# Causal mask of the transposed scores: a minimum on VectorE for a product on TensorE, and the value products a slot later

## Chip, core and metric

One core of a Trainium2 chip runs the whole program. The metric is the device time of one execution, in microseconds (us). The engines are named as in the profile: PE is TensorE, DVE is VectorE, ACT is ScalarE, POOL is GpSimd, SP is SyncE, which here only issues DMAs.

## Reference

One transformer layer with a mixture of experts: attention with 16 heads of 8 columns over 16 sequences of 256 tokens, a layer norm, a top-1 choice among 8 experts, and a second layer norm. Cut to what matters here (written together, in the reference's terms):

```python
x = L0_attn_x                                        # (16, 256, 128), f32
q, k, v = (x @ w + b).reshape(B, S, 16, 8)           # for wq, wk, wv; then RoPE on q and k
scores = einsum('bhqd,bhkd->bhqk', q, k) / sqrt(8)
causal = where(tril(ones((S, S))) == 0, -1000000000.0, 0.0)
attn = softmax(scores + causal, axis=-1)
x = layernorm(x + einsum('bhqk,bhkd->bhqd', attn, v) @ wo + bo)
# top-1 of 8 experts, each takes at most T // 8 = 512 tokens in order; T = 4096
# (the shapes follow the reference's routing; tokens over the limit get zero)
out = gate * kept * (x @ W[e].T + b[e])
return layernorm(x + out)
```

## Kernel before

The work is cut by sequence. A sequence of 256 tokens passes through five stages, and a **step** s works on five or six sequences at once, each in another stage: n = s + 2 (projections and rotation), a = s + 1 and b = s (row maxima of the scores), c = s - 1 (scores again, exponentials, products with the values), d = s - 2 (norm, output projection, routing, experts), e = s - 3 (the last norm and output). There are 20 steps, s = -2 to 17; steps 1 to 16 have a sequence c.

Every step is cut into **slots** (14 of them, `SLOTS`), and each engine's program is the same loop over the slots with its own work written under them. That hand-written order is all that sets what an engine does next: no engine takes anything out of turn, and they meet in semaphores. Work that stands in an earlier slot is ahead in the queue of its engine, and in one slot the order is that of the code.

Attention is computed twice over. The first pass computes scores with a query a row and takes the row maxima (DVE, line 725), in eleven **chunks** k of up to 512 columns (`CHUNKS`). Each is a mask product (`masks`, line 898, with `mask_a_bf`), then products of the rotated queries and keys (line 924) into one of the two banks `ps_a`; PE waits in `a_taken` until DVE has taken chunk k - 2. The second pass computes the scores transposed, in the same eleven chunks, with the maxima already subtracted by extra rows of the product: a mask product (line 898, with `mask_b_bf`), which adds -3e9 where a key is behind its query, the products (line 914) into one of the two banks `ps_b`, and the exponential on ACT into one of the `PR` buffers of `probs` (line 544). Blocks have 64 tokens, so in each group of a chunk only the first 64 columns, the diagonal block, hold masked elements: 8 chunks have two groups (128 mask columns), 2 have four (256), the last has eight (512). Products of `probs` with the values (line 936, called PV k here) add up in `ps_pv`; a column of ones among the values gives the sums.

Chunk k of the second pass stands in slot k + 2 (`B_SLOT`), PV k in slot k + 3 (`PV_SLOT`). The maxima of b stand in the slots that `MAXIMA_IN` names, its chunk 2 in slot 0, chunk 3 in slot 2, chunk 4 in slot 3 and so on; chunks 0 and 1 of a are in the last two slots (`EARLY`). DVE has, besides the maxima: the reciprocals of the sums (lines 735, 737), attn (line 742), the choice of the largest among the experts' results (`select`, line 711), the residual sums and statistics (lines 704, 749, 691, 695), the splitting of x and of the normed rows (lines 763, 767), routing (lines 772 to 821) and the rotation products (lines 798, 801). POOL has the splitting of the rotated rows and maxima, the copies into `v_diag` and the reciprocal roots.

Of the kernel before, what the change touches and what calls it, by code (L numbers as in the profile page):

```python
# [27 lines left out]
B, S, D = 16, 256, 128  # L28
# [5 lines left out]
BLK = 64  # L34
# [18 lines left out]
NCH = len(CHUNKS)  # L53
B_SLOT, PV_SLOT, SLOTS = 2, 3, NCH + 3
EARLY = 2
# [3 lines left out]
def _layout():  # L59
    at = 0  # L60
    for name, w in (("ident", 128), ("before", 128), ("cos", S), ("sin", S), ("mask_a", BLK), ("mask_b", BLK),
                    ("stacked", BLK), ("head_cols", PH * HD), ("head_is", PH), ("tie", E), ("max_sel", H // 2)):
        CONSTS[name] = (at, w)
        at += w
    return at
# [23 lines left out]
def layer_kernel(nc, x, wq, bq, wk, bk, wv, bv, wo, bo, wg, W, b, const, expert_rows, out):  # L89
# [8 lines left out]
    with ExitStack() as ctx:  # L98
# [22 lines left out]
        out_bias = sb("out_bias", [128, 128])  # L121
        PR = 3
        probs = sb("probs", [128, PR, 512])
# [9 lines left out]
        ident_bf = sb("ident_bf", [128, 128], bf)  # L133
        mask_a_bf, mask_b_bf = sb("mask_a_bf", [128, BLK], bf), sb("mask_b_bf", [128, BLK], bf)
        stacked_bf = sb("stacked_bf", [128, BLK], bf)
# [64 lines left out]

        names += """b_ready exp_done pv_ready""".split()

# [286 lines left out]
        def _(act):  # L489
# [29 lines left out]
            def narrow_tables():  # L519

                act.wait_ge(s_["tables_loaded"], 16)
                for to, name in ((ident_bf, "ident"), (mask_a_bf, "mask_a"), (mask_b_bf, "mask_b"), (stacked_bf, "stacked"),
                                 (before_bf, "before")):
                    last = act.activation(to[:, :], C(name), ACT.Copy)
                last.then_inc(s_["consts_done"], 1)
# [8 lines left out]
            def step(s, p, half):  # L534
                n, a, b, c, d = s + 2, s + 1, s, s - 1, s - 2
                for slot in range(SLOTS):
# [31 lines left out]
                    if slot == 11 and has(b):  # L568
# [9 lines left out]
                        for half_at in range(2):  # L578
                            act.dma_start(q_plain[p][SCORE_ROWS:SCORE_ROWS + MAX_ROWS, 4 * half_at:4 * half_at + 4, :],
                                          max_rows[MAX_ROWS * half_at:MAX_ROWS * half_at + MAX_ROWS, :].unsqueeze(1)  # L580
                                          .broadcast_to([MAX_ROWS, 4, S])).then_inc(s_["maxrows_loaded"], 16)
                    if slot == 13 and has(c):
                        after(act, "pv_ready", c, NCH, NCH)
# [13 lines left out]
        def _(dve):  # L597
# [116 lines left out]
            def step(s, p, half):  # L714
                n, a, b, c, d, e = s + 2, s + 1, s, s - 1, s - 2, s - 3
                for slot in range(SLOTS):
                    for t, k in maxima_at(slot, a, b):
                        after(dve, "a_ready", t, NCH, k + 1)
# [12 lines left out]
                    if slot == 3 and has(e):  # L731
                        select(e, 1)
                    if slot == 13 and has(c):
                        after(dve, "sums_copied", c, 1, 1)
                        dve.reciprocal(inv_den[:, 0:128], sums[:, 0:128]).then_inc(s_["den_done"], 1)  # L735
# [101 lines left out]
        def _(pe):  # L837
# [62 lines left out]
            def step(s, p, half):  # L900
                n, a, b, c, d = s + 2, s + 1, s, s - 1, s - 2
                q = 1 - p
                for slot in range(SLOTS):
                    k = slot - B_SLOT
                    if has(c) and 0 <= k < NCH:
# [5 lines left out]
                        after(pe, "exp_done", c, NCH, k - 1)  # L911
                        masks(ps_b[k % 2], CHUNKS[k], mask_b_bf, False)
                        for j, g, col in parts_of(CHUNKS[k]):
                            mm = pe.matmul(ps_b[k % 2][:, col:col + width(j)], diag_block(k_diag[q], g, j),  # L914
                                           q_plain[q][:, g, BLK * j:S], start=False, stop=True, skip_group_check=True)
                        mm.then_inc(s_["b_ready"], 1)
# [23 lines left out]
                    if slot == 11 and has(b):  # L940
# [82 lines left out]
def constants():  # L1023
# [50 lines left out]
```

## Time and profile before

| what | value |
|---|---|
| time, median of 3 runs | 451.69 us (450.78 to 453.25) |
| profiled execution, its own time | 453.58 us |
| span of the profile | 451.9 us |
| PE busy | 407.0 us (90%) |
| DVE busy | 316.2 us (70%) |
| POOL busy | 202.9 us (45%) |
| ACT busy | 173.6 us (38%) |
| mean granted clock of PE | 0.947 of full speed |

The span runs from the first to the last instruction of the profiled execution; its own time is 1.7 us more. The busy share is a mean over start, middle and end: the middle, where all stages are full, is the part to read by windows. Matmuls are pipelined, so the length of one in the trace is longer than its share of PE: what one costs is the distance from its start to the start of the next. On DVE too the next instruction can start a little (some 0.08 us) before the end of the one ahead. A PE product of 4-byte data is two records in the trace.

### The profile page before, as it was taken

How to read it: one execution, taken by the hardware profiler on the slowest of the kernel's cores; microseconds unless marked ns; L12 is line 12 of the kernel's file. 1: busy time of each engine (PE TensorE's matmuls, PEld its weight loads, DVE VectorE, ACT ScalarE, POOL GpSimd, SP SyncE). 2: the span in 40 equal slices, each digit the busy share in tenths (PEclk: the TensorE clock that was granted, in tenths of full speed). 3: DMA queues.
4: the chain of work that ended last, by engine and by line, in shares of the span. 5: the costliest groups of instructions: out<-in, count | busy, mean ns of one | idle time of the engine just before them, and what ended most of it. 6: DMA issues, size and time to landing. Idle time of an engine off the chain costs nothing. (4 is left out here: it accounts for less than half of the span.)

```text
span 451.9 us, 10461 instructions
## 1 busy us (share of the span) xinstructions
PE 407.0 (90%) x3270; PEld 356.6 (79%) x3270; DVE 316.2 (70%) x814; ACT 173.6 (38%) x377; POOL 202.9 (45%) x376
## 2 busy tenths in 40 slices
PE   5363798999999999999999999999999999999842
PEld 4352687989898898989898989898898988897731
DVE  5567544768786878878787778786868877755553
ACT  7541234343444434434434343434434343435300
POOL 6265133333635354463646363635354555151313
PEclk9658696999999999999999999999999999999958
DMA  5399663928468684939393939587586759600000
GB/s 142 75 197 147 117 85 81 158 62 141 87 121 123 126 114 119 122 101 147 86 162 84 148 81 153 88 144 97 128 114 134 98 130 108 95 10 23 13 0 24
DMA packets 145828, 47.29 MB, mean 105 GB/s; under 512 B 104350, under 2 KB 142114, under 8 KB 145803
## 3 DMA queue, kind: packets, MB, share of 16 engines
q1 hardware_dynamic: 139898, 42.65, 58.1%
q10 hardware_dynamic: 5184, 2.36, 2.8%
q0 software_dynamic: 720, 1.97, 1.5%
q8 instruction: 13, 0.21, 0.2%
q14 instruction: 13, 0.10, 0.1%
HBM read 30.70 MB, written 14.68 MB: 100 GB/s over the span
## 5 line engine op out<-in xcount | busy, mean ns | idle before, releaser
L936 PE MATMUL ps_pv<-probs,v_diag 128*128 128x64 f32 (+3 forms) x1024 | 192.8, 324 | 2.9 <-ACT probs L544 2.4
L936 PEld LDWEIGHTS ps_pv<-probs,v_diag 128*128 128x128 f32 x1024 | 147.6, 193 | 12.6 <-ACT probs L544 6.7
L544 ACT ACTIVATE probs<-ps_ab 128x512 f32<-128x512 f32 (+1 forms) x176 | 97.8, 559 | 153.6 <-PE ps_ab L914 149.2
L725 DVE TENSOR_REDUCE row_max<-ps_ab 128x2 f32<-128x512 f32 (+3 forms) x176 | 107.9, 631 | 20.3 <-PE ps_ab L924 20.1
L924 PE MATMUL ps_ab<-k_plain,q_diag 128*128 128x64 bf16 (+3 forms) x512 | 67.0, 241 | 0.0
L914 PE MATMUL ps_ab<-q_plain,k_diag 128*128 128x64 bf16 (+3 forms) x512 | 65.3, 236 | 0.0
L898 PE MATMUL ps_ab<-mask_a_bf,ident_bf 128*128 128x128 bf16 (+2 forms) x176 | 44.6, 253 | 11.7 <-DMA q_diag<-plain_parts 8.1
L711 DVE TENSOR_REDUCE y_sel<-ps_m 128x128 f32<-128x1024 f32 x31 | 37.8, 1219 | 14.2 <-PE ps_m L887 14.2
L437 POOL COPY v_diag<-v_rows 64x128 f32<-64x128 f32 x64 | 18.4, 288 | 64.8 <-ACT v_rows L566 62.8
L898 PE MATMUL ps_ab<-mask_b_bf,ident_bf 128*128 128x128 bf16 (+2 forms) x176 | 43.7, 248 | 0.0
L914 PEld LDWEIGHTS ps_ab<-q_plain,k_diag 128*128 128x128 bf16 x512 | 36.1, 99 | 8.2 <-issue 0.6
L735 DVE RECIPROCAL inv_den<-sums 128x128 f32<-128x128 f32 x16 | 15.2, 953 | 37.1 <-ACT sums L508 37.1
L375 POOL TENSOR_SCALAR rs<-mv 128x2 f32<-128x2 f32 x32 | 7.3, 230 | 74.3 <-DVE mv L695 74.3
L924 PEld LDWEIGHTS ps_ab<-k_plain,q_diag 128*128 128x128 bf16 x512 | 37.0, 101 | 3.4
L898 PEld LDWEIGHTS ps_ab<-mask_a_bf,ident_bf 128*128 128x128 bf16 x176 | 17.9, 102 | 21.5 <-DVE row_max L725 7.8
L469 POOL TENSOR_TENSOR rot_rest<-rot 128x512 f32<-128x512 f32 x15 | 17.6, 1174 | 35.4 <-ACT rot L590 35.4
L798 DVE SCALAR_TENSOR_TENSOR rot_cs<-ps_m,bias_cols,cst 128x256 f32<-128x256 f32 x32 | 15.3, 479 | 17.6 <-PE ps_m L869 17.6
L867 PE MATMUL ps_m<-we_hi,x1t_hi 128*128 128x512 f32 x62 | 27.6, 445 | 0.0
L867 PE MATMUL ps_m<-xt_hi,w_hi 128*128 128x256 f32 x64 | 21.2, 331 | 4.7 <-DVE xt_lo L767 4.7
L466 POOL TENSOR_TENSOR rot<-rot_cs 128x512 f32<-128x512 f32 x15 | 19.4, 1296 | 13.1 <-DVE rot_cs L801 11.4
L386 POOL TENSOR_SCALAR y_out<-z,mv,rs 128x128 f32<-128x128 f32 x30 | 23.8, 795 | 3.4 <-POOL rs L377 3.4
L868 PE MATMUL ps_m<-we_lo,x1t_hi 128*128 128x512 f32 x62 | 25.0, 403 | 0.0
(156 smaller groups left out, 726.1 us busy)
## 6 DMA issues: line engine op xcount, KB each, us to landing
plain_parts<-rot SPq DMA_DIRECT2D x180, 64.0 KB, 2.0
k_plain<-plain_parts SPq DMA_DIRECT2D x16, 384.0 KB, 3.8
q_diag<-plain_parts SPq DMA_DIRECT2D x32, 192.0 KB, 5.3
q_plain<-plain_parts SPq DMA_DIRECT2D x16, 384.0 KB, 5.9
k_diag<-plain_parts SPq DMA_DIRECT2D x32, 192.0 KB, 6.6
x_in<-in_L_attn_x_dram SPq DMA_DIRECT2D x16, 128.0 KB, 5.9
x_res<-in_L_attn_x_dram SPq DMA_DIRECT2D x16, 128.0 KB, 3.0
out_dram<-y_out POOLq DMA_DIRECT2D x15, 128.0 KB, 2.6
```

Of the source, the lines that this page charges most:

```text
L386: last = pool.tensor_scalar(y_out[:, t, :], z2[:, t, :], mv2[:, t, 0:1], rs2[:, t:t + 1], ALU.subtract, ALU.mult)
L437: last = pool.tensor_copy(dst[:, :, :, HD * hl:HD * hl + HD], src[:, :, :, HD * hl:HD * hl + HD])
L466: pool.tensor_tensor(rot[:, :, :], rot_c[:, :, :], rot_s[:, :, :], ALU.add).then_inc(s_["rot_done"], 1)
L544: act.activation(probs[:, k % PR, 0:cols], ps_b[k % 2][:, 0:cols], ACT.Exp, scale=SCALE)\
L711: dve.tensor_reduce(y_sel[:, t, :], expert_bank(d, t)[:, :, :].rearrange("p a (e f) -> p f (a e)", e=4), AX.X, ALU.max).then_inc(s_["moe_t ...
L725: last = dve.tensor_reduce(row_max[:, NBLK - 1 - j, groups[0]:groups[-1] + 1], scores[:, :, col:col + width(j)], AX.X, ALU.max)
L867: pe.matmul(out, sh, mh, start=start, stop=False, skip_group_check=True)
L868: pe.matmul(out, sh, ml, start=False, stop=False, skip_group_check=True)
L898: return pe.matmul(v, ident_bf[:, :], rows, start=True, stop=False, skip_group_check=True)
L914: mm = pe.matmul(ps_b[k % 2][:, col:col + width(j)], diag_block(k_diag[q], g, j), q_plain[q][:, g, BLK * j:S], start=False, stop=True, ski ...
L924: mm = pe.matmul(maxima_bank(t, k)[:, col:col + width(j)], diag_block(q_diag[at], g, NBLK - 1 - j), k_plain[at][:, g, 0:width(j)], start=F ...
L936: mm = pe.matmul(ps_pv[:, g // 4, BLK * j:S], v_diag[q][:, j, 128 * g:128 * g + 128], probs[:, k % PR, col:col + width(j)], start=(j == 0 ...
```

## The change

The mask of the second pass is no longer added to the scores by a PE product. The first product of each chunk now starts the bank, the exponential is taken of the unmasked scores, and DVE then replaces the diagonal blocks in `probs` by their minimum with a table `keep_b` that holds 0 where a key is behind its query and 2^100 elsewhere. There is one such instruction a chunk, in slot k + 3 and first in it, behind a wait for the chunk's exponential; it has two inputs in SBUF. PV k waits for it (`cut_done`) and stands in slot k + 4. `probs` has four buffers for three, and a step has 15 slots for 14: what stood in the last slot (13) stands in slot 14, and the early maxima of a in slots 13 and 14. The mask of the first pass stays.

```diff
--- before.py
+++ after.py
@@ -51,14 +51,14 @@
 CHUNKS = [((j,), (2 * h, 2 * h + 1)) for j in range(2) for h in range(4)]
 CHUNKS += [((2,), (0, 1, 2, 3)), ((2,), (4, 5, 6, 7)), ((3,), tuple(range(PAIRS)))]
 NCH = len(CHUNKS)
-B_SLOT, PV_SLOT, SLOTS = 2, 3, NCH + 3
+B_SLOT, PV_SLOT, SLOTS = 2, 4, NCH + 4
 EARLY = 2
 MAXIMA_IN = {0: (2,), 2: (3,), 3: (4,), 4: (5,), 5: (6,), 6: (7,), 7: (8,), 8: (9, 10)}
 
 CONSTS = {}
 def _layout():
     at = 0
-    for name, w in (("ident", 128), ("before", 128), ("cos", S), ("sin", S), ("mask_a", BLK), ("mask_b", BLK),
+    for name, w in (("ident", 128), ("before", 128), ("cos", S), ("sin", S), ("mask_a", BLK), ("keep_b", BLK),
                     ("stacked", BLK), ("head_cols", PH * HD), ("head_is", PH), ("tie", E), ("max_sel", H // 2)):
         CONSTS[name] = (at, w)
         at += w
...
@@ -119,7 +119,7 @@
         bv_wide = sb("bv_wide", [128, 128])
         wo_in = sb("wo_in", [128, 128])
         out_bias = sb("out_bias", [128, 128])
-        PR = 3
+        PR = 4
         probs = sb("probs", [128, PR, 512])
         w_exp = probs[:, 0:2, :].rearrange("p a (e f) -> p (a e) f", f=128)
         we_hi, we_lo = sb("we_hi", [128, E, 128], fr), sb("we_lo", [128, E, 128], fr)
...
@@ -714,6 +714,14 @@
             def step(s, p, half):
                 n, a, b, c, d, e = s + 2, s + 1, s, s - 1, s - 2, s - 3
                 for slot in range(SLOTS):
+                    k = slot - B_SLOT - 1
+                    if has(c) and 0 <= k < NCH:
+                        after(dve, "exp_done", c, NCH, k + 1)
+                        dve.nop(nofuse=True)
+                        diagonal = probs[:, k % PR, 0:columns_of(CHUNKS[k])]\
+                            .rearrange("p (g x) -> p g x", g=len(CHUNKS[k][1]))[:, :, 0:BLK]
+                        dve.tensor_tensor(diagonal, diagonal, C("keep_b").unsqueeze(1).broadcast_to([128, len(CHUNKS[k][1]), BLK]),
+                                          ALU.min).then_inc(s_["cut_done"], 1)
                     for t, k in maxima_at(slot, a, b):
                         after(dve, "a_ready", t, NCH, k + 1)
                         if k == 0:
...
@@ -909,10 +917,9 @@
                                 pe.wait_ge(s_["start_act"], 4)
                             after(pe, "maxrows_loaded", c, 2 * 16, 2 * 16)
                         after(pe, "exp_done", c, NCH, k - 1)
-                        masks(ps_b[k % 2], CHUNKS[k], mask_b_bf, False)
-                        for j, g, col in parts_of(CHUNKS[k]):
+                        for i, (j, g, col) in enumerate(parts_of(CHUNKS[k])):
                             mm = pe.matmul(ps_b[k % 2][:, col:col + width(j)], diag_block(k_diag[q], g, j),
-                                           q_plain[q][:, g, BLK * j:S], start=False, stop=True, skip_group_check=True)
+                                           q_plain[q][:, g, BLK * j:S], start=(i == 0), stop=True, skip_group_check=True)
                         mm.then_inc(s_["b_ready"], 1)
                     for t, k in maxima_at(slot, a, b):
                         at = p if t is b else q
...
@@ -928,7 +935,7 @@
                         experts(d, n, 0)
                     k = slot - PV_SLOT
                     if has(c) and 0 <= k < NCH:
-                        after(pe, "exp_done", c, NCH, k + 1)
+                        after(pe, "cut_done", c, NCH, k + 1)
                         if k == 0:
                             after(pe, "v_done", c, 1, 1)
                             after(pe, "pv_copied", c)
...
@@ -946,7 +953,7 @@
                                            max_parts[:, 2 * i:2 * i + 2, :].rearrange("p i m -> p (i m)"), stacked_bf[:, :],
                                            start=(i == 0), stop=True, skip_group_check=True)
                         mm.then_inc(s_["ex_ready"], 1)
-                    if slot == 13 and has(d):
+                    if slot == SLOTS - 1 and has(d):
                         experts(d, n, 1)
                     if slot == 4 and has(d):
                         after(pe, "normed", d, 1, 1)
...
-    put("mask_b", np.where(col[None, :] < r[:, None], NEG, 0.0))
+    put("keep_b", np.where(col[None, :] < r[:, None], 0.0, BIG))
```

Left out are the same renaming at two tables, the new semaphore's name, and the three places where slot 13 has become `SLOTS - 1` (the copies of sums and weighted values on ACT, the first half reciprocal on DVE, the second half of the experts on PE).

PE, before, from the maxima of chunk 4 (slot 3) on: a mask (L898) and products of scores, value products L936, the product with wo L955.

```order
L898 MATMUL ps_ab<-mask_a_bf,ident_bf 128x2x64 [waits a_taken]
L924 MATMUL ps_ab<-k_plain,q_diag 128x192 x2
L936 MATMUL ps_pv<-probs,v_diag 128x256 [waits pv_copied,v_done,exp_done]
L936 MATMUL ps_pv<-probs,v_diag 128x256
L898 MATMUL ps_ab<-mask_b_bf,ident_bf 128x2x64 [waits exp_done]
L914 MATMUL ps_ab<-q_plain,k_diag 128x256 x2
L898 MATMUL ps_ab<-mask_a_bf,ident_bf 128x2x64 [waits a_taken]
L924 MATMUL ps_ab<-k_plain,q_diag 128x192 x2
L936 MATMUL ps_pv<-probs,v_diag 128x256 [waits exp_done]
L936 MATMUL ps_pv<-probs,v_diag 128x256
L955 MATMUL ps_n<-wo_in,attn 128x128 [waits maxrows_done,normed]
L955 MATMUL ps_n<-wo_in,attn 128x128
```

And PE, after, from the same chunk (line numbers are those of the changed kernel: L906 is the mask, L931 and L921 the score products, L943 the value products, L962 the one with wo).

```order
L906 MATMUL ps_ab<-mask_a_bf,ident_bf 128x2x64 [waits a_taken]
L931 MATMUL ps_ab<-k_plain,q_diag 128x192 x2
L921 MATMUL ps_ab<-q_plain,k_diag 128x256 [waits exp_done]
L921 MATMUL ps_ab<-q_plain,k_diag 128x256
L906 MATMUL ps_ab<-mask_a_bf,ident_bf 128x2x64 [waits a_taken]
L931 MATMUL ps_ab<-k_plain,q_diag 128x192 x2
L943 MATMUL ps_pv<-probs,v_diag 128x256 [waits pv_copied,v_done,cut_done]
L943 MATMUL ps_pv<-probs,v_diag 128x256
L962 MATMUL ps_n<-wo_in,attn 128x128 [waits maxrows_done,normed]
L962 MATMUL ps_n<-wo_in,attn 128x128
L921 MATMUL ps_ab<-q_plain,k_diag 128x256 [waits exp_done]
L921 MATMUL ps_ab<-q_plain,k_diag 128x256
```

Between the maxima of chunk 4 and those of chunk 5 PE had the first value product and a chunk of transposed scores; it now has the scores alone, and the first value product stands behind chunk 5.

DVE, before, slots 2 to 5: attn, the maxima of chunk 4, `select`, the maxima of chunk 5, residual sums, statistics, the maxima of chunk 6.

```order
L742 TENSOR_TENSOR attn<-weighted,inv_den 128x256 [waits den_done,y_ready,pv_copied]
L725 TENSOR_REDUCE row_max<-ps_ab 128x2 [waits a_ready]
L711 TENSOR_REDUCE y_sel<-ps_m 128x128 [waits moe_ready]
L725 TENSOR_REDUCE row_max<-ps_ab 128x2 [waits a_ready]
L704 SCALAR_TENSOR_TENSOR z<-y_sel,gate_kept,x 128x128 [waits gk_done,moe_taken,out_done]
L704 SCALAR_TENSOR_TENSOR z<-y_sel,gate_kept,x 128x128 [waits gk_done,moe_taken]
L749 TENSOR_TENSOR z<-ps_n,x_bias 128x256 [waits xb_done,y_ready]
L691 BN_STATS st<-z 128x6 [waits z1_done]
L691 BN_STATS st<-z 128x6
L695 BN_AGGR mv<-st 128x2 [waits st1_done] x2
L725 TENSOR_REDUCE row_max<-ps_ab 128x2 [waits a_ready]
```

DVE, after, the same stretch; L723 is the minimum, L733 the maxima, L750 attn.

```order
L750 TENSOR_TENSOR attn<-weighted,inv_den 128x256 [waits den_done,y_ready,pv_copied]
L723 TENSOR_TENSOR probs<-probs,cst 128x2x64 [waits exp_done]
L733 TENSOR_REDUCE row_max<-ps_ab 128x2 [waits a_ready]
L711 TENSOR_REDUCE y_sel<-ps_m 128x128 [waits moe_ready]
L723 TENSOR_TENSOR probs<-probs,cst 128x2x64 [waits exp_done]
L733 TENSOR_REDUCE row_max<-ps_ab 128x2 [waits a_ready]
L704 SCALAR_TENSOR_TENSOR z<-y_sel,gate_kept,x 128x128 [waits gk_done,moe_taken,out_done]
L704 SCALAR_TENSOR_TENSOR z<-y_sel,gate_kept,x 128x128 [waits gk_done,moe_taken]
L757 TENSOR_TENSOR z<-ps_n,x_bias 128x256 [waits xb_done,y_ready]
L691 BN_STATS st<-z 128x6 [waits z1_done]
L691 BN_STATS st<-z 128x6
L695 BN_AGGR mv<-st 128x2 [waits st1_done] x2
```

Minimum 0 stands in front of the maxima of chunk 4, minimum 1 behind `select`, and minimum 2 (the row behind the last one shown) behind the statistics.

DVE, before, slots 11 to 13: statistics, the early maxima of a, `select`, the half reciprocal.

```order
L691 BN_STATS st<-z 128x6 [waits z2_done]
L691 BN_STATS st<-z 128x6
L695 BN_AGGR mv<-st 128x2 [waits st2_done] x2
L725 TENSOR_REDUCE row_max<-ps_ab 128x2 [waits widened,a_ready]
L711 TENSOR_REDUCE y_sel<-ps_m 128x128 [waits moe_ready]
L725 TENSOR_REDUCE row_max<-ps_ab 128x2 [waits a_ready]
L735 RECIPROCAL inv_den<-sums 128x128 [waits sums_copied]
```

DVE, after, slots 11 to 14.

```order
L723 TENSOR_TENSOR probs<-probs,cst 128x4x64 [waits exp_done]
L691 BN_STATS st<-z 128x6 [waits z2_done]
L691 BN_STATS st<-z 128x6
L695 BN_AGGR mv<-st 128x2 [waits st2_done] x2
L723 TENSOR_TENSOR probs<-probs,cst 128x4x64 [waits exp_done]
L711 TENSOR_REDUCE y_sel<-ps_m 128x128 [waits moe_ready]
L723 TENSOR_TENSOR probs<-probs,cst 128x512 [waits exp_done]
L733 TENSOR_REDUCE row_max<-ps_ab 128x2 [waits widened,a_ready]
L733 TENSOR_REDUCE row_max<-ps_ab 128x2 [waits a_ready]
L743 RECIPROCAL inv_den<-sums 128x128 [waits sums_copied]
```

The minima of chunks 8 and 9 stand around the statistics, the last one directly behind `select`, and both early maxima behind it.

## Rows read from the trace of the kernel before

**Rows 1.** Busy time by window, twelve steps; columns: PE, PEld, DVE, ACT, POOL, clock, DMA.
```profile
97.36:385.64 288.28, 287.72 (x2423) 254.74 (x2422) 221.79 (x571) 116.00 (x263) 142.52 (x273) 1.00 0.71 118
```

**Rows 2.** Timeline of DVE: the first half reciprocal, once a step (start, us).
```profile
97.36 0.95 DVE L735 RECIPROCAL inv_den<-sums 128x128 f32<-128x128 f32 x1 [2.35 <-ACT sums L508]
```

**Rows 3.** Timeline of PE, slots 0 to 7 of the step from 195.02.
```profile
195.02 0.23 PE L898 MATMUL ps_ab<-mask_a_bf,ident_bf 128*128 128x128 bf16 x1
...
195.31 0.22 PE L898 MATMUL ps_ab<-mask_b_bf,ident_bf 128*128 128x128 bf16 x1
195.36 0.38 PE L914 MATMUL ps_ab<-q_plain,k_diag 128*128 128x256 bf16 x2
...
196.25 0.23 PE L898 MATMUL ps_ab<-mask_a_bf,ident_bf 128*128 128x128 bf16 x1
...
196.51 1.13 PE L936 MATMUL ps_pv<-probs,v_diag 128*128 128x256 f32 x4
197.48 0.22 PE L898 MATMUL ps_ab<-mask_b_bf,ident_bf 128*128 128x128 bf16 x1
...
197.75 0.22 PE L898 MATMUL ps_ab<-mask_a_bf,ident_bf 128*128 128x128 bf16 x1
...
201.84 0.41 PE L867 MATMUL ps_m<-w_hi,xt_hi 128*128 128x128 f32 x1
...
202.89 0.22 PE L898 MATMUL ps_ab<-mask_b_bf,ident_bf 128*128 128x128 bf16 x1
```

**Rows 4.** Timeline of DVE in the same slots.
```profile
196.12 0.94 DVE L737 RECIPROCAL inv_den<-sums 128x128 f32<-128x128 f32 x1
196.98 0.63 DVE L725 TENSOR_REDUCE row_max<-ps_ab 128x2 f32<-128x512 f32 x1
197.52 0.41 DVE L742 TENSOR_TENSOR attn<-weighted,inv_den 128x256 f32<-128x256 f32 x1
197.85 0.55 DVE L725 TENSOR_REDUCE row_max<-ps_ab 128x2 f32<-128x384 f32 x1
198.31 1.21 DVE L711 TENSOR_REDUCE y_sel<-ps_m 128x128 f32<-128x1024 f32 x1
199.44 0.55 DVE L725 TENSOR_REDUCE row_max<-ps_ab 128x2 f32<-128x384 f32 x1
...
201.58 0.56 DVE L725 TENSOR_REDUCE row_max<-ps_ab 128x2 f32<-128x384 f32 x1
202.89 0.60 DVE L757 TENSOR_SCALAR x<-z,mv,rs 128x128 f32<-128x128 f32 x2 [0.75 <-POOL rs L377]
```

**Rows 5.** Groups by form: DVE instructions with two SBUF inputs.
```profile
L704 DVE SCALAR_TENSOR_TENSOR z<-y_sel,gate_kept,x 128x128 f32<-128x128 f32 x32 | 9.6, 342 | 0.0
...
L742 DVE TENSOR_TENSOR attn<-weighted,inv_den 128x256 f32<-128x256 f32 x16 | 6.9, 434 | 0.3
...
L777 DVE TENSOR_TENSOR below<-logits,top 128x16 f32<-128x16 f32 x16 | 3.5, 218 | 0.5
```

**Rows 6.** Source view: one tiny DVE instruction with two SBUF inputs; min/median/max.
```profile
L821 DVE TENSOR_TENSOR gate_kept<-n_kept,gate x16: 160/820/915, 90.3 to 439.0; 128x2 f32<-128x2 f32 x16
```

**Rows 7.** Timeline: the POOL sum and the DVE product beside it.
```profile
186.90 1.30 POOL L466 TENSOR_TENSOR rot<-rot_cs 128x512 f32<-128x512 f32 x1 [0.16 <-POOL seen L462]
...
187.31 0.92 DVE L821 TENSOR_TENSOR gate_kept<-n_kept,gate 128x2 f32<-128x2 f32 x1
```

**Rows 8.** Timeline of DVE, slots 10 to 12 of the step before.
```profile
184.87 0.48 DVE L798 SCALAR_TENSOR_TENSOR rot_cs<-ps_m,bias_cols,cst 128x256 f32<-128x256 f32 x1 [0.80 <-PE ps_m L869]
...
188.14 0.47 DVE L691 BATCH_NORM_STATS2 st<-z 128x6 f32<-128x128 f32 x2
...
190.13 1.22 DVE L711 TENSOR_REDUCE y_sel<-ps_m 128x128 f32<-128x1024 f32 x1 [0.54 <-PE ps_m L887]
```

**Rows 9.** Timeline of PE over the same slots.
```profile
184.67 0.28 PE L898 MATMUL ps_ab<-mask_b_bf,ident_bf 128*128 128x256 bf16 x1
...
191.27 2.00 PE L936 MATMUL ps_pv<-probs,v_diag 128*128 128x64 f32 x16
```

More of the change, by code:

```diff
@@ L133, in layer_kernel @@
         ident_bf = sb("ident_bf", [128, 128], bf)
-        mask_a_bf, mask_b_bf = sb("mask_a_bf", [128, BLK], bf), sb("mask_b_bf", [128, BLK], bf)
+        mask_a_bf = sb("mask_a_bf", [128, BLK], bf)
         stacked_bf = sb("stacked_bf", [128, BLK], bf)
@@ L199, in layer_kernel @@
         names += """a_ready a_taken widened parted ex_ready maxrows_done v_ready vrows_done v_done""".split()
-        names += """b_ready exp_done pv_ready""".split()
+        names += """b_ready exp_done cut_done pv_ready""".split()
         names += """pv_copied sums_copied den_done normed xb_done y_ready z1_done st1_done mv1_done ve1_done
@@ L521, in narrow_tables @@
                 act.wait_ge(s_["tables_loaded"], 16)
-                for to, name in ((ident_bf, "ident"), (mask_a_bf, "mask_a"), (mask_b_bf, "mask_b"), (stacked_bf, "stacked"),
+                for to, name in ((ident_bf, "ident"), (mask_a_bf, "mask_a"), (stacked_bf, "stacked"),
                                  (before_bf, "before")):
@@ L581, in step @@
                                           .broadcast_to([MAX_ROWS, 4, S])).then_inc(s_["maxrows_loaded"], 16)
-                    if slot == 13 and has(c):
+                    if slot == SLOTS - 1 and has(c):
                         after(act, "pv_ready", c, NCH, NCH)
@@ L732, in step @@
                         select(e, 1)
-                    if slot == 13 and has(c):
+                    if slot == SLOTS - 1 and has(c):
                         after(dve, "sums_copied", c, 1, 1)
```

## Prediction

> **What bounds the kernel now.** I read the busy time by window first. Over twelve whole steps, 97.36 to 385.64 us, PE is busy 287.7 of 288.3 us at a granted clock of 1.00, DVE 221.8 and POOL 142.5 [rows 1]. The window runs from one half reciprocal [rows 2] to the twelfth after it, which comes once a step, so a step (one sequence through every stage) lasts 288.28 / 12 = 24.02 us, of which DVE works 18.5. So PE's own work and its few waits set the step, and DVE has 5.5 us over. That margin is not free time at will: both engines run in program order and hand chunks to each other, so I went on to the timelines of PE and DVE over one step and set the waits of the changed order against them. Time zero below is 195.02, where PE issues maxima chunk 2 at the start of a step (slot 0) [rows 3].
>
> In slots 0 to 4 PE already meets DVE. The maxima banks are two, so PE's chunk 4 waits until DVE has taken chunk 2: it is issued at 196.25, and chunk 5 at 197.75 [rows 3], just behind DVE's reduction of chunk 3, which starts at 196.98 and takes 0.63, to 197.61 [rows 4]. DVE is late there because of the second half reciprocal, 0.94 us from 196.12 [rows 4]. What PE does meanwhile is the first product with the values (PV 0), from 196.51 to 197.48 [rows 3].
>
> **What goes.** Eleven mask products a step. The mask of 128 columns moves the next product from 195.31 to 195.36 [rows 3], 0.05 us, although its own span reads 0.22. Eight chunks have 128 mask columns, two 256, one 512: 2048 columns, 16 x 0.053 = 0.85 us a step, 13.6 us in 16 steps. That is all that PE can gain. The narrowing of the mask table at the start also goes; it is off any path there.
>
> **What comes on DVE.** Eleven minima a step with two SBUF inputs, none of which is in the trace. The nearest rows: 0.342 us for 128 x 128 with a scalar besides, 0.434 for 128 x 256 (0.41 where nothing disturbs it), 0.218 for 128 x 16 [rows 4, 5]. Fixed 0.18 and some 0.9 ns a column give 0.29, 0.41 and 0.66 us for 128, 256 and 512 columns: 8 x 0.29 + 2 x 0.41 + 0.66 = 3.8 us a step. From below it is 11 x 0.2 = 2.2, from above 8 x 0.34 + 2 x 0.43 + 1.0 = 4.6; I take 3.8, since it rests on rows on both sides. Each waits for an exponential behind a no-operation, so nothing of it overlaps the instruction ahead. DVE's work becomes 18.5 + 3.8 = 22.3 us, and its waits (2.35 us for the sums alone [rows 2]) do not all shrink. A step of 23.2 us (24.02 - 0.85) would need them under 1 us.
>
> **What moves: slots 2 to 6.** I replay the new order with these durations. PE reaches chunk 4 at 1.23 as before. PV 0 is now behind the next slot's score product and maxima chunk 5, and chunk 5 cannot start before DVE has taken chunk 3, at 2.59 (197.61). So PE stands idle from 1.7 to 2.6 where PV 0 was. DVE then does attn (197.52 plus 0.41, to 2.91), and only then minimum 0, to 3.24; PV 0 starts at 3.3 instead of 1.5, and with PV 0's 0.9 and the product with wo behind it (some 0.4, an estimate from its four products of 128 columns beside the four of 256) PE is through at 4.6. Minimum 1 stands behind chunk 4 and the 1.21 us selection of experts [rows 4]: DVE reaches it at 4.87, PV 1 goes at 5.2 to 6.1. Minimum 2 stands behind chunk 5, the residual sums and the norm statistics. That stretch of DVE is 199.44 to 201.58 now [rows 4], 2.14 us; begun at 5.1 it ends at 7.3, and minimum 2 at 7.6. PE has finished two more score and maxima chunks by 6.5 and waits 1.1 us for it. PV 2 (some 0.7) and the value projection with the transposes (201.84 to 202.89, 1.05 [rows 3]) follow: PE is at the head of slot 7 at 9.4. Before, it is there at 202.89 - 195.02 = 7.87 [rows 3], and with PV 3 already done. So this stretch is 1.5 us later and still owes a PV of 0.9.
>
> **Slots 7 to 14.** Up to the projections (slot 9) PE and DVE go hand in hand, at 13.85 for PE, with 0.1 us of wait. From their end to PV 10 DVE has the rotation products (begin 0.2 after the end of the projections), routing, a minimum of 0.41, statistics, a minimum of 0.41, the selection (1.22) and the last minimum of 0.66. Rows now: 184.87 to 188.90 (the statistics begin at 188.14 and take 0.76) is 4.03 [rows 8]; 0.2 + 4.03 + 0.41 + 0.41 + 1.2 + 0.66 and 0.2 of joints are 7.1 us. PE needs from 184.67 to 191.27 now, 6.6 [rows 9], less masks (0.43) and a wait (0.17), plus one more PV (0.6): 6.6 again. So PE waits another 0.5 us before PV 10. The expert products, and the sums that wait for PV 10, follow as now. Against now this half gains 0.43 + 0.16 of masks and 0.17 of the old wait, and loses 0.9 (the PV owed), 0.1 and 0.5: +0.7.
>
> A step is thus 24.1 + 1.5 + 0.7 = 26.3 us, +2.2. DVE would be busy 22.3 of it, PE some 22.8.
>
> **POOL.** A tiny DVE product with two SBUF inputs takes 160 ns at least and 820 in the median [rows 6]. In rows it starts at 187.31 and ends at 188.23, right behind the end (188.20) of a POOL sum that began before it [rows 7]. So a two-input DVE instruction that meets a working POOL ends with it, and the minima are of that kind. POOL works 142.5 of 288.3 us, half the time [rows 1]. On my replayed times minimum 10 (at 21.8) meets the splitting of the rotated rows on POOL and minima 6 and 7 meet short ones; the others fall in POOL's pauses or beside waits. I take 0.2 us a step on the path, with bounds 0 and 1.5. The Trainium skill, page "SBUF — State Buffer", section "SBUF: two separate sides", states the rule against this change: the port pair that VectorE and GpSimd share is an exclusive lock, held for a whole instruction, which a VectorE instruction with two SBUF inputs takes too, and "the other fully blocks". By that rule the trace agrees in the one pair shown; a sum without it would leave the 0.2 out.
>
> **The sum.** Thirteen steps are as full on both engines as these twelve (the one ahead of them is): 13 x (2.2 + 0.2) = 31 us. The two or three steps at the end have no maxima and no projections; PE wins 0.85 in each and waits for minima 1 and 2 behind the same DVE work, between -1.7 and +2 together; I take 0. Start and tail have no minima: 0. The extra slot by itself is only order. The profiled execution took 453.6 us, span 451.9; it becomes 453.6 + 31 = 485. It stood 1.9 above the median of 451.7, so I predict 483 us.
>
> **Own range.** With minima at 0.2 us each DVE reaches minimum 2 0.25 sooner and the last one 0.9 sooner, so the second wait goes and a step costs +1.3: 13 x 1.3 - 1.7 = +15, 467. With the high prices and 0.6 for POOL it is 3.4: 13 x 3.4 + 2 = +46, 498.
>
> **Rivals.** (a) PE stays the bound and DVE's 5.5 us take in the 3.8: then 453.6 - 13.6 - 1.9 = 438 us, faster. For it: PE is at 99.8% and DVE at 77% [rows 1]. Against: it needs PV 2 not to wait, that is minimum 2 ready by 6.5, and DVE's queue puts it at 7.6. It decides at that place: were all three early minima ahead of DVE's other work, this would be the case. 0.06. (b) The waits come but only eat the masks' 0.85 us: a step stays at 24, 452 us. It needs the idle time at chunk 5 (0.9) to be all, with the minima under way while DVE now idles. 0.05. (c) The lock is met by most minima. A POOL instruction lasts 142.5 / 273 = 0.52 us in the mean and the long ones 1.2 to 1.3 [rows 1, 7], so a meeting costs some 0.4; 11 x 0.49 x 0.4 = 2.2 us a step, all on a DVE without slack: 13 x 4.4 = 57, 508 us. Against: DVE and POOL have a chain of their own in which they take turns, so meetings aren't random. 0.07. The Trainium skill's page of above is what makes (c) a rule and not an accident of one row. (d) The forecast: 0.82.
>
> The range that holds 8 in 10 is 463 to 499: (d)'s own with a little below it; (a) and most of (c) are left out. Faster by over 0.5% (what a measurement of this kernel can tell from no change) has (a) and a little of (b), 0.07; within 0.5% 0.04; slower 0.89.
>
> **What would show it.** In the profile after: steps of 26 to 27 us between the same reciprocals; DVE busy 22 to 23 us a step, over 83%, and PE down to 86 to 88%; minima of 0.29, 0.41 and 0.66 us; three new waits of PE a step, for DVE's reduction before chunk 5 (0.9), for minimum 0 (0.4) and for minimum 2 (1.1), and one of 0.5 before PV 10. POOL's share in it shows as minima longer than those figures. I am wrong if PE still is busy 99% of the middle steps, if PV 2 finds its minimum ready, or if the minima's median is far from 0.3 us.

## The result and the profile after

The changed kernel takes 489.12 us (median of 4 runs, 487.63 to 490.72) against 451.24 us before (4 runs): ratio 1.082, interval 1.077 to 1.086. It is 37.9 us slower; 483 was forecast, with 463 to 499 as range. The profiled execution took 490.13 us. From its page, the span and the busy times:

```profile
span 488.5 us, 10524 instructions
...
PE 408.4 (84%) x3094; PEld 346.1 (71%) x3094; DVE 372.5 (76%) x990; ACT 172.2 (35%) x376; POOL 210.3 (43%) x376
```

Busy time by window, from one first half reciprocal to the eleventh after it (columns as in [rows 1]):

```profile
97.89:394.99 297.10, 266.81 (x2114) 227.31 (x2112) 245.60 (x649) 106.17 (x243) 135.59 (x249) 0.99 0.67 105
```

The twelve steps of [rows 1] are not the same stretch: in the last of them there are no projections any more, and it lasts 22.50 us. The same eleven steps of the kernel before, and then the three at the end (from the eleventh to the last first half reciprocal), before and after:

```profile
97.36:363.14 265.78, 265.30 (x2235) 235.18 (x2234) 205.34 (x528) 107.18 (x243) 130.56 (x250) 1.00 0.71 118
363.14:426.76 63.62, 63.09 (x512) 54.88 (x511) 41.22 (x117) 25.57 (x58) 25.37 (x53) 1.00 0.41 64
```

```profile
394.99:463.70 68.71, 62.70 (x479) 52.84 (x478) 49.94 (x149) 25.42 (x58) 26.48 (x52) 1.00 0.36 58
```

So a full step lasts 297.10 / 11 = 27.01 us, 2.85 more than 265.78 / 11 = 24.16, and the three steps at the end together 5.1 us more. DVE is busy 245.6 / 11 = 22.3 us of a full step, where it was 18.7; PE is busy 90% of it, where it was 100%. POOL's instructions are the same, but its busy time is 12.3 us a step for 11.9.

The groups by form: the minima, new, and attn, whose row before is in [rows 5]:

```profile
L723 DVE TENSOR_TENSOR probs<-probs,cst 128x128 f32<-128x128 f32 x128 | 36.8, 289 | 0.1
...
L723 DVE TENSOR_TENSOR probs<-probs,cst 128x512 f32<-128x512 f32 x16 | 16.6, 1040 | 6.5 <-ACT probs L544 6.5
...
L723 DVE TENSOR_TENSOR probs<-probs,cst 128x256 f32<-128x256 f32 x32 | 14.3, 453 | 0.0
...
L750 DVE TENSOR_TENSOR attn<-weighted,inv_den 128x256 f32<-128x256 f32 x16 | 10.4, 648 | 0.3
```

128 and 256 columns take 0.29 and 0.45 us, next to the forecast 0.29 and 0.41. The minimum of chunk 10 takes 1.04, not 0.66, and attn has gone from 0.434 to 0.648 though nothing about it was changed.

Timeline of PE over the step that begins at 180.40 (start us, us, engine, line), the answer to [rows 3]; what it waited for is in the brackets:

```profile
181.64 0.23 PE L906 MATMUL ps_ab<-mask_a_bf,ident_bf 128*128 128x128 bf16 x1
...
183.04 0.23 PE L906 MATMUL ps_ab<-mask_a_bf,ident_bf 128*128 128x128 bf16 x1 [0.79 <-DVE row_max L733]
...
183.98 1.13 PE L943 MATMUL ps_pv<-probs,v_diag 128*128 128x256 f32 x4 [0.55 <-DVE probs L723]
...
185.84 1.08 PE L943 MATMUL ps_pv<-probs,v_diag 128*128 128x256 f32 x4
...
188.12 1.13 PE L943 MATMUL ps_pv<-probs,v_diag 128*128 128x256 f32 x4 [0.82 <-DVE probs L723]
...
189.95 0.33 PE L921 MATMUL ps_ab<-q_plain,k_diag 128*128 128x192 bf16 x2
...
202.57 0.22 PE L906 MATMUL ps_ab<-mask_a_bf,ident_bf 128*128 128x128 bf16 x1
...
203.51 2.00 PE L943 MATMUL ps_pv<-probs,v_diag 128*128 128x64 f32 x16 [0.50 <-DVE probs L723]
```

And of DVE, the answer to [rows 4] and [rows 8]:

```profile
182.90 0.83 DVE L750 TENSOR_TENSOR attn<-weighted,inv_den 128x256 f32<-128x256 f32 x1
183.65 0.28 DVE L723 TENSOR_TENSOR probs<-probs,cst 128x128 f32<-128x128 f32 x1
...
187.78 0.29 DVE L723 TENSOR_TENSOR probs<-probs,cst 128x128 f32<-128x128 f32 x1
...
200.24 0.43 DVE L723 TENSOR_TENSOR probs<-probs,cst 128x256 f32<-128x256 f32 x1
200.72 1.22 DVE L711 TENSOR_REDUCE y_sel<-ps_m 128x128 f32<-128x1024 f32 x1
202.31 1.15 DVE L723 TENSOR_TENSOR probs<-probs,cst 128x512 f32<-128x512 f32 x1 [0.37 <-ACT probs L544]
```

PE issues chunk 5 of the maxima at 183.04, 0.95 us after it was through with the score products ahead of it. (The bracket says 0.79: the record of a product runs on some 0.16 us after PE could take the next one, so the busy share hides that much of each wait.) PV 0 starts at 183.98, 0.72 after PE was through with chunk 5, right behind the first minimum, which waits behind attn. PV 2 starts at 188.12, 0.99 late, behind the minimum at 187.78, which stands behind the statistics. PV 10 starts at 203.51, 0.67 after the early maxima (202.57, and 0.27 for their products), behind the minimum of chunk 10. Those four waits sum to 3.3 us. Slot 7 begins at 189.95 - 180.40 = 9.55; it was 7.87 in [rows 3], and the replay said 9.4.

Two rows of POOL and three of ACT say why the long ones are long:

```profile
182.70 0.73 POOL L415 TENSOR_TENSOR x_bias<-x_res,out_bias 128x256 f32<-128x256 f32 x1
...
201.74 1.16 POOL L469 TENSOR_TENSOR rot_rest<-rot 128x512 f32<-128x512 f32 x1 [2.46 <-ACT rot L590]
```

```profile
199.21 1.62 ACTq L579 DMA_DIRECT2D q_plain<-max_rows  x2
200.95 0.63 ACT L590 ACTIVATE rot<-rot 128x512 bf16<-128x512 f32 x1 [1.77 <-issue]
201.61 0.60 ACT L544 ACTIVATE probs<-ps_ab 128x512 f32<-128x512 f32 x1
```

Attn started at 182.90 and ended at 183.73, where POOL's sum ended at 183.43. The last minimum came 0.37 us late to begin with, since the exponential of chunk 10 stood on ACT behind two DMA issues (1.62 us) and the copy of the rotated rows; it then ended at 203.46, 0.56 after POOL's subtraction (202.90), which had begun before it. Neither ends with POOL's instruction: each goes on for most of its own length behind it.

### The profile page after: what moved, and what is told of

Read it like the earlier page. It is cut to its first block, busy times and chain, and to the rows that moved or that the text cites. A ratio compares the mean times of both kernels' runs of the same rounds, so it can differ in the third digit from the quotient of the medians.

```text
span 488.5 us, 10524 instructions
## 1 busy us (share of the span) xinstructions
PE 408.4 (84%) x3094; PEld 346.1 (71%) x3094; DVE 372.5 (76%) x990; ACT 172.2 (35%) x376; POOL 210.3 (43%) x376
## 4 chain that ended last, share of the span: by engine, by line
PE 57%; DVE 25%; issue 8%; ACT 4%; DMA 2%; ACTq 1%; SPq 1%; DVEq 1%; POOL 1%; POOLq 0%
PE ps_pv L943 23%; PE ps_m L875 5%; DVE probs L723 5%; PE ps_m L877 5%; PE ps_m L876 5%; DVE row_max L733 5%; PE ps_ab L931 4%; PE ps_ab L921 4%; DVE y_sel L711 3%; ACT probs L544 3%; PE ps_m L895 3%; PE ps_ab L906 2%; DVE z L704 2%; DVE inv_den L745 1%; ACTq L579 1%
## 5 line engine op out<-in xcount | busy, mean ns | idle before, releaser
L943 PE MATMUL ps_pv<-probs,v_diag 128*128 128x64 f32 (+3 forms) x1024 | 194.6, 326 | 25.1 <-DVE probs L723 24.6
L943 PEld LDWEIGHTS ps_pv<-probs,v_diag 128*128 128x128 f32 x1024 | 147.7, 193 | 41.4 <-DVE probs L723 36.1
L544 ACT ACTIVATE probs<-ps_ab 128x512 f32<-128x512 f32 (+1 forms) x176 | 96.7, 559 | 169.4 <-PE ps_ab L921 164.4
L733 DVE TENSOR_REDUCE row_max<-ps_ab 128x2 f32<-128x512 f32 (+3 forms) x176 | 107.7, 630 | 15.9 <-PE ps_ab L931 15.4
L723 DVE TENSOR_TENSOR probs<-probs,cst 128x128 f32<-128x128 f32 (+2 forms) x176 | 67.8, 387 | 6.7 <-ACT probs L544 6.5
L931 PE MATMUL ps_ab<-k_plain,q_diag 128*128 128x64 bf16 (+3 forms) x512 | 67.6, 243 | 0.0
L921 PE MATMUL ps_ab<-q_plain,k_diag 128*128 128x64 bf16 (+3 forms) x512 | 66.4, 238 | 0.5 <-ACT probs L544 0.5
L906 PE MATMUL ps_ab<-mask_a_bf,ident_bf 128*128 128x128 bf16 (+2 forms) x176 | 45.0, 256 | 23.8 <-DVE row_max L733 14.7
L906 PEld LDWEIGHTS ps_ab<-mask_a_bf,ident_bf 128*128 128x128 bf16 x176 | 18.1, 103 | 37.5 <-DVE row_max L733 24.4
L921 PEld LDWEIGHTS ps_ab<-q_plain,k_diag 128*128 128x128 bf16 x512 | 37.2, 99 | 7.3 <-ACT probs L544 0.7
L931 PEld LDWEIGHTS ps_ab<-k_plain,q_diag 128*128 128x128 bf16 x512 | 37.4, 102 | 3.7
L386 POOL TENSOR_SCALAR y_out<-z,mv,rs 128x128 f32<-128x128 f32 x30 | 25.3, 847 | 3.4 <-POOL rs L377 3.4
L507 ACT ACTIVATE sums<-ps_pv 64x256 f32<-64x256 f32 x16 | 6.1, 381 | 56.0 <-PE ps_pv L943 56.0
L877 PE MATMUL ps_m<-we_hi,x1t_lo 128*128 128x512 f32 x62 | 25.0, 403 | 0.0
```

The source lines that it names most:

```text
L386: last = pool.tensor_scalar(y_out[:, t, :], z2[:, t, :], mv2[:, t, 0:1], rs2[:, t:t + 1], ALU.subtract, ALU.mult)
L544: act.activation(probs[:, k % PR, 0:cols], ps_b[k % 2][:, 0:cols], ACT.Exp, scale=SCALE)\
L723: dve.tensor_tensor(diagonal, diagonal, C("keep_b").unsqueeze(1).broadcast_to([128, len(CHUNKS[k][1]), BLK]), ALU.min).then_inc(s_["cut_do ...
L733: last = dve.tensor_reduce(row_max[:, NBLK - 1 - j, groups[0]:groups[-1] + 1], scores[:, :, col:col + width(j)], AX.X, ALU.max)
L877: return pe.matmul(out, sl, mh, start=False, stop=stop, skip_group_check=True)
L906: return pe.matmul(v, ident_bf[:, :], rows, start=True, stop=False, skip_group_check=True)
```

## The experiments

Each is timed beside the kernel before on one chip, but not all on the same one, so among themselves they are best compared by ratios and steps. Step lengths are read in one profiled execution of each, as above, over the same eleven full steps. The short diffs are against the kernel named.

| kernel | median us | ratio to before (interval) | step us |
|---|---|---|---|
| before | 451.2 to 452.6 | 1 | 24.16 |
| changed | 489.1 | 1.082 (1.077 to 1.086) | 27.01 |
| shift alone | 460.6 | 1.021 (1.018 to 1.025) | 24.94 |
| minima, no shift | 584.7 | 1.295 (1.291 to 1.300) | 32.94 |
| changed, no mask at all | 456.7 | 1.012 (1.007 to 1.017) | 24.65 |
| changed, minima on a spare buffer | 470.7 | 1.043 (1.040 to 1.045) | 25.69 |
| changed, minima 1 and 2 early | 487.0 | 1.078 (1.074 to 1.083) | 26.69 |
| changed, exponential 10 early | 474.8 | 1.051 (1.047 to 1.054) | 25.84 |
| changed, short POOL | 477.0 | 1.056 (1.052 to 1.060) | 26.18 |
| changed, mask product too | 493.5 | 1.092 (1.087 to 1.097) | 27.09 |
| before, exponential 10 early | 445.9 | 0.985 (0.981 to 0.989) | 23.88 |
| that, minimum for chunk 10 | 442.6 | 0.979 (0.975 to 0.982) | 23.65 |
| that, minima for 8, 9, 10 | 445.7 | 0.987 (0.982 to 0.991) | 23.96 |

**The shift alone.** From the kernel before:

```diff
-B_SLOT, PV_SLOT, SLOTS = 2, 3, NCH + 3
+B_SLOT, PV_SLOT, SLOTS = 2, 4, NCH + 4
-        PR = 3
+        PR = 4
```

> The kernel before with the products with the values one slot later (four buffers of probs, 15 slots), the mask product kept on PE and no minima. Theory A (the minima are late in DVE's queue, and PV 0 no longer fills PE's wait for DVE before maxima chunk 5): only the second half of it acts, some +0.7 us a step, about +9 us, 461 us. Rival B (DVE's added work alone is what costs): no change, 452 us. Rival C (the shift is what costs): the whole loss, 480 to 489 us.

460.6 us and +0.78 a step: theory A's number. The waits of PE from 95 to 385 us (total, times, longest) show it; the view lists none of this kind for the kernel before:

```profile
PE ps_ab L898 <- DVE row_max L725: 8.4, 12, 0.7
```

Attn takes 0.62 us in the mean in this kernel, where it was 0.43, without a single minimum: the shift alone already brings it beside POOL's sum.

**Minima without the shift.** From the changed kernel, `PV_SLOT` back to 3 with 14 slots and `PR = 3`.

> The changed kernel with PV k back in slot k + 3 (14 slots, three buffers), so each minimum and its product stand in one slot. Theory A: PV 0 to PV 2 still wait for minima that stand behind DVE's other work, and in the later slots score product, exponential, minimum and value product form one chain in a slot: slower than the changed kernel, about 500 us. Rival C: back near the kernel before or under it, 440 to 455 us.

584.7 us, 8.8 more a step than the kernel before. The direction is A's, the size is not: 500 was far off. Rival C is out. By window, and the one wait of PE that the view lists in it:

```profile
95.00:385.00 290.00, 226.01 (x1676) 188.68 (x1675) 193.24 (x512) 84.57 (x193) 107.40 (x193) 0.96 0.55 86
```

```profile
PE ps_pv L943 <- DVE probs L723: 63.4, 70, 2.2
```

PE is busy 226 of 290 us and DVE 193, so neither works at its limit, and PE waits 70 times for a minimum, up to 2.2 us: in a slot score product, exponential, minimum and value product follow one another, with DVE's other work in between. (The third buffer fewer was not tried by itself.) The later slot for PV is needed once the minima are there; it costs 0.78 of its own.

**No mask, and minima that nobody waits for.** Both from the changed kernel, the first without the minima, the second with them on a buffer of their own:

```diff
-                        after(pe, "cut_done", c, NCH, k + 1)
+                        after(pe, "exp_done", c, NCH, k + 1)
```

> The changed kernel without the minima (PV k waits for the exponential): the mask of the transposed scores is left out altogether. Theory A: PE's gain of 0.85 us a step comes, less what goes into the wait before chunk 5, against the +0.7 of the shift: 451 us, within 4. Rival C: still 475 us or more. A clock or PE-side cause would show here as well.

> The changed kernel with the same eleven minima in the same places, after the same wait for the exponential, but on a spare buffer, and PV k waits for the exponential only; the mask of the transposed scores is left out. DVE has all the added work, PE does not wait for it. Theory A: the dependence is most of the loss, some 456 us, at most 465. Rival B (DVE has become the bound by its busy time): near the changed kernel, 480 to 489 us.

Without any mask the kernel takes 456.7, outside the 451 within 4. A's gain for PE was too large: of 0.85 us that PE no longer works, 0.29 a step are won over the shift alone. The rest goes into waits, as at chunk 5, which is issued 0.95 us after the products ahead of it are through (195.33 + 0.22):

```profile
195.33 0.38 PE L913 MATMUL ps_ab<-q_plain,k_diag 128*128 128x256 bf16 x2
196.50 0.23 PE L898 MATMUL ps_ab<-mask_a_bf,ident_bf 128*128 128x128 bf16 x1 [0.79 <-DVE row_max L725]
```

With the minima as load alone it is 470.7, above A's bound of 465 and far below B's 480: DVE's added time costs 1.04 us a step, its being waited for 1.32 more. Both theories had a part. DVE is busy 22.6 us a step in that kernel, and its added work reaches PE through the banks of the maxima. By window over the eleven steps, then that wait of PE from 95 to 385 us, first in this kernel and then in the one without any mask:

```profile
94.77:377.31 282.54, 264.10 (x2114) 223.70 (x2113) 248.88 (x649) 106.31 (x243) 135.42 (x250) 1.00 0.71 111
```

```profile
PE ps_ab L910 <- DVE row_max L737: 15.8, 32, 0.8
```

```profile
PE ps_ab L898 <- DVE row_max L725: 9.7, 13, 0.8
```

**Two minima early.** From the changed kernel, minimum 1 before the selection, minimum 2 before the residual sums:

```diff
+                    if has(c) and slot in (B_SLOT + 1, B_SLOT + 2):
+                        cut(slot - B_SLOT)
```

> The changed kernel with two of the eleven minima moved ahead on DVE: minimum 1 stands before the selection of experts and minimum 2 before the residual sums and the norm statistics (each behind the row maxima of the slot before). The same work on every engine. Theory A (where the minima stand in DVE's queue): PE's wait of 0.99 us for minimum 2 goes, other work of DVE is later by 0.3 to 0.6; step -0.7 to -1.0, 475 to 480 us. Rival B (DVE's busy time): no change, 489.

487.0: a step is only 0.3 shorter, not 0.7 to 1.0. PV 2 does start 0.17 after the products ahead of it, without a wait, but PV 3 now waits (PE first, then DVE):

```profile
183.32 0.33 PE L936 MATMUL ps_ab<-k_plain,q_diag 128*128 128x192 bf16 x2
183.49 1.05 PE L948 MATMUL ps_pv<-probs,v_diag 128*128 128x256 f32 x4
...
186.53 1.13 PE L948 MATMUL ps_pv<-probs,v_diag 128*128 128x256 f32 x4 [0.63 <-DVE probs L721]
```

```profile
185.68 0.60 DVE L770 TENSOR_SCALAR x<-z,mv,rs 128x128 f32<-128x128 f32 x2 [0.76 <-POOL rs L377]
186.19 0.28 DVE L721 TENSOR_TENSOR probs<-probs,cst 128x128 f32<-128x128 f32 x1
```

The minimum of chunk 3 stands behind x1, and x1 behind POOL's reciprocal root. The wait has moved to the next product. I read this as the whole stretch of DVE up to x1 being too long for what PE has to do beside it, whatever the place of one minimum; no run shortens that stretch.

**Exponential 10 early.** From the changed kernel, ACT alone:

```diff
-                    if has(c) and 0 <= k < NCH:
+                    if has(c) and 0 <= k < NCH - 1:
                         exponential(k)
+                    if has(c) and slot == B_SLOT + NCH - 2:
+                        exponential(NCH - 1)
```

> The changed kernel with the exponential of chunk 10 moved ahead on ACT, before the copy of the maxima rows, its two DMA issues and the copy of the rotated rows. In the trace the exponential starts 2.8 us after its scores are done, minimum 10 waits 0.37 for it, then runs 1.15 us beside POOL's split, and PE waits 0.72 before PV 10. If ACT's queue is the cause of that wait it goes: -0.5 to -0.7 a step, 480 to 482 us. If DVE's queue or the port lock are, under -0.2 a step, 487 to 489.

474.8 us, 14 less, more than the most expected. DVE and PE in it, and POOL's residual sum:

```profile
193.11 0.68 DVE L728 TENSOR_TENSOR probs<-probs,cst 128x512 f32<-128x512 f32 x1
...
200.27 0.41 DVE L755 TENSOR_TENSOR attn<-weighted,inv_den 128x256 f32<-128x256 f32 x1
```

```profile
193.88 0.38 PE L936 MATMUL ps_ab<-k_plain,q_diag 128*128 128x256 bf16 x2
194.10 1.90 PE L948 MATMUL ps_pv<-probs,v_diag 128*128 128x64 f32 x16
...
200.93 1.13 PE L948 MATMUL ps_pv<-probs,v_diag 128*128 128x256 f32 x4
...
205.15 1.13 PE L948 MATMUL ps_pv<-probs,v_diag 128*128 128x256 f32 x4 [0.90 <-DVE probs L728]
```

```profile
201.15 0.74 POOL L415 TENSOR_TENSOR x_bias<-x_res,out_bias 128x256 f32<-128x256 f32 x1
```

The minimum takes 0.68 (it starts before POOL's subtraction, which begins at 193.65), PV 10 follows the early maxima at 0.22 with no wait, and attn is at 0.41 again, since POOL's residual sum now comes after it. That shortens PE's wait before PV 0 too: chunk 5 is issued at 200.41 and PV 0 at 200.93, 0.52 later, where it was 0.94. So of the 1.17 us a step 0.67 are the wait before PV 10 and 0.42 the one before PV 0. PV 2's wait has stayed (0.90 in the bracket).

**Short POOL.** From the changed kernel, four POOL instructions on 8 columns (one of them shown):

```diff
-pool.tensor_tensor(rot_rest[:, :, :], rot[:, :, :], rot_1[:, :, :], ALU.subtract)
+pool.tensor_tensor(rot_rest[:, :, 0:8], rot[:, :, 0:8], rot_1[:, :, 0:8], ALU.subtract)
```

> The changed kernel with four POOL instructions a step cut to 8 columns (the sum of residual and bias, the split of the rotated rows in three); the rest of these rows is left out. If a two-input DVE instruction waits for POOL's: attn falls from 0.83 to 0.41 and minimum 10 from 1.1 to 0.68, PE's waits for both shrink as much, -0.8 a step, 477 to 480 us. If the length has another cause (size, stride) both stay and the time is 488 to 490.

477.0 us, as expected of a wait for POOL. The forms:

```profile
L724 DVE TENSOR_TENSOR probs<-probs,cst 128x512 f32<-128x512 f32 x16 | 11.2, 699 | 6.7 <-ACT probs L545 6.7
...
L751 DVE TENSOR_TENSOR attn<-weighted,inv_den 128x256 f32<-128x256 f32 x16 | 6.6, 410 | 0.3
```

Same minimum, same place, same late exponential (6.7 us of waits), and 0.70 us where it was 1.04; attn 0.41 for 0.65. The length was a wait for POOL and not size or stride. With the exponential still late, PV 10 now starts 0.20 us after PE is through with the early maxima, so of the 0.67 in the changed kernel some 0.47 were the meeting with POOL and 0.20 the late exponential.

**Both masks.** From the changed kernel, the product with `mask_b_bf` back ahead of the scores.

> The changed kernel with the mask product of the transposed scores put back on PE, so that the mask is applied twice. PE has its 0.85 us a step again, DVE and all waits are unchanged. If PE in the changed kernel mostly waits for DVE, the products run inside those waits: 489 to 493 us, under a third of the 13.6 us that they cost in PE time. If PE still were the bound: 500 us or more.

493.5 us, 4.4 more than the changed kernel and just above the forecast 489 to 493. By window over the eleven steps:

```profile
97.17:395.21 298.04, 273.35 (x2235) 234.33 (x2234) 247.10 (x649) 106.81 (x243) 135.78 (x249) 1.00 0.65 105
```

A full step is 0.09 us longer, with 0.85 us more of products in it; PE's busy time grows by 0.6 a step. So in the full steps nine tenths of PE's gain were spent waiting. The two profiled executions differ by 2.5 us, of which the full steps make 0.9.

**A faster version.** Exponential 10 early in the kernel before; then, on top, the minimum in place of the mask product for chunk 10 only, at the head of DVE's slot 12; then for chunks 8 and 9 too, all with PV in slot k + 3.

```diff
-                        masks(ps_b[k % 2], CHUNKS[k], mask_b_bf, False)
+                        if k not in CUT:
+                            masks(ps_b[k % 2], CHUNKS[k], mask_b_bf, False)
```

> The kernel before with the exponential of chunk 10 moved ahead on ACT in the same way. PE waits 0.3 us a step before PV 10 for it (3.4 us in eleven steps on its weight loads, less for the products). It should win 0.15 to 0.3 a step, 447 to 449 us; if the DMA issue and the rotated rows that are now later by 0.6 matter, 452 or more.

> The kernel before with the exponential of chunk 10 early on ACT (446 us measured), and the minimum on DVE instead of the mask product for chunk 10 alone (512 mask columns), placed at the start of slot 12 on DVE; PV k stays in slot k + 3. PE wins 0.21 us a step, DVE has 0.66 more where it has room: 442 to 444 us. If any work on DVE costs, 446 or more.

> The same with the minima of chunks 8, 9 and 10 (1024 of the 2048 mask columns), minimum 8 between the two pairs of rotation products and minimum 9 before the statistics of slot 11. PE wins 0.43 us a step, DVE has 1.5 more: 439 to 441 us. If minimum 8 is late for PV 8, or the rotation and routing behind it matter, 444 to 450.

The first gives 445.9, 1.5% under the kernel before and 1 us better than the best expected, with 0.28 a step; PE's wait for that exponential is gone. The second gives 442.6, as expected: 0.23 more a step, for 0.21 of mask product. It is the fastest run here, 2.1% under the kernel before; against the first the intervals of the ratios just overlap, so the gain of the minimum rests on the step length. The third misses: 445.7, 0.31 a step more than the second, where 0.22 less was forecast. PE, then DVE:

```profile
181.10 1.16 PE L965 MATMUL ps_pv<-probs,v_diag 128*128 128x128 f32 x8
182.38 0.22 PE L974 MATMUL ps_n<-stacked_bf,max_parts 128*128 128x64 bf16 x2
```

```profile
180.62 0.43 DVE L730 TENSOR_TENSOR probs<-probs,cst 128x256 f32<-128x256 f32 x1
...
182.08 0.15 DVE L835 SCALAR_TENSOR_TENSOR kept<-ps_n,chosen_f 128x16 f32<-128x16 f32 x1
```

Minimum 8 stands among the rotation products and is done at 181.05; PV 8, ready at 180.94, starts at 181.10. All behind it on DVE is later by 0.5, so the routing result is there at 182.23 and the product that waits for it (182.38) is some 0.3 late. The two waits are more than the masks' time.

## Why the prediction held, and where it did not

The direction and its cause held. PE's 0.85 us a step was not won; the waits are where the replay put them, and DVE's work is the 22.3 us of the sum. By its steps:

- **The wait before chunk 5** (0.9 forecast) is 0.95, and the shift alone shows that it comes, at +0.78 a step, without a single minimum.
- **PV 0 behind minimum 0** was forecast as 0.4 and is 0.72. The term that was mis-sized is the lock: I kept attn at 0.41, since it meets no POOL work in the kernel before; here it takes 0.83 in the step shown.
- **PV 2 behind minimum 2** was forecast as 1.1 and is 0.99.
- **PV 10 behind the last minimum** was forecast as 0.5 and is 0.67, for a wrong reason. I added up DVE's queue up to it. In the trace DVE was idle ahead of it and waited for ACT, and then for POOL; without the 0.37 and 0.47 us of these it would have ended at 202.62 (an estimate from the rows above), before PE was ready at 202.84. The move of one exponential on ACT takes the whole wait away, with DVE's queue as it was. The step that failed is "PE waits another 0.5 us before PV 10" as DVE's sum: I had not set ACT's queue (two DMA issues and a copy ahead of that exponential) against the new order. That the number came near was luck.
- **POOL** was put at 0.2 us a step and is worth up to 0.83 (27.01 to 26.18 with its long instructions short). That is between my figure and rival (c)'s 2.2; most minima do miss POOL. The rule that I took from one pair, that such an instruction ends with POOL's, is too cheap: the pair was a tiny product, and attn and minimum 10 end 0.30 and 0.56 us after POOL's.
- **Overlap.** I had the minima start only behind the end of the instruction ahead. Where the exponential was long done they start 0.08 before it: minimum 0 at 183.65, with attn ending at 183.73.
- **Size.** 485 was forecast for the profiled execution and it took 490.1. The thirteen steps were put at 31 us and cost 31.9, but by errors that cancel: each of the eleven measured above costs 2.85 and not 2.2 + 0.2 (31.3 us), while the two ahead of them, start included, cost only 0.5 together. The term that was mis-sized in the total is the end, put at 0 with +2 as its bound: the last three steps cost 5.1. They do not lack the maxima, as I had it: two of the three still have maxima, and PE's waits between 394.99 and 463.70 are of the kinds of a full step:

```profile
PE ps_pv L943 <- DVE probs L723: 3.1, 6, 0.8
PE ps_ab L906 <- DVE row_max L733: 1.6, 2, 0.8
```

Of the signs given, DVE is busy 83% and PE 90%, where 86 to 88% was said; the minima up to 256 columns and the three early waits are there. Rival (a), PE remaining the bound, needed minimum 2 in time for PV 2. Rival (b), waits that only eat the masks' 0.85 us, needed the wait before chunk 5 to be all; it is 0.95 of 3.3. The steps of the sequence before, shift, no mask, unawaited minima, changed are +0.78, -0.29, +1.04 and +1.32 us, +2.85 together.

Not settled: how much of the 1.17 us that the early exponential wins in the changed kernel is ACT's order itself. The short POOL alone wins 0.83, at the same two products (PV 0 and PV 10), so an estimate for ACT's part is 1.17 - 0.83 = 0.3 us. Both changes together were not run. What minima with the same work, but one SBUF input, would cost was not tried.

## What to carry to other kernels

Work moved from a full engine to one with a margin pays only if the receiver's queue has it done where it is needed; count the receiver's wait-free stretch against the giver's, slot by slot, and not the busy shares. A mask product of 512 columns was worth moving (0.23 us a step won for 0.69 on VectorE at a place with room); moving all eleven mask products was not. Compare steps over the same stretch of both kernels: a mean that takes in one step of the end was 0.14 us too low here. And look for what stands ahead of the one instruction that everybody waits for: one exponential moved ahead of two DMA issues gave 1.5% by itself.

## What the runs showed of the hardware

A VectorE instruction with two SBUF inputs is drawn out when a GpSimd instruction is under way: the same minimum takes 1.04 us in the mean beside GpSimd's subtraction and 0.70 with that cut short, attn 0.65 and 0.41, and a step 0.83 us less. Minima of 128 columns, which mostly meet no GpSimd work, keep their 0.29. It goes the other way too: GpSimd's cast behind the subtraction takes 0.90 us in the mean in the changed kernel, where it begins before the last minimum ends, and 0.66 before:

```profile
L473 POOL CAST rot<-rot_rest 128x512 bf16<-128x512 f32 x15 | 13.5, 901 | 2.0
```

The Trainium skill, page "SBUF — State Buffer", section "SBUF: two separate sides", has the shared port pair as an exclusive lock, held for the whole instruction by whichever starts first. The runs agree: attn and the last minimum end 0.30 and 0.56 us after the GpSimd instruction, most of the 0.41 and 0.68 that they take alone.

A DMA issue on ScalarE holds up what stands behind it: two took 1.62 us here (from 199.21), and the copy and the exponential behind them started at 200.95 and 201.61.
